# Where the repeated reciprocals of small-head attention are transposed, and in which order the first attention takes its query tiles

## The reference

```
q, k, v = projections of x          # layers 0 and 1: with rotary embedding
scores  = q @ k.T * scale           # layer 1: plus a bias by head and distance
scores  = where(causal, scores, -inf)
out     = softmax(scores) @ v       # per head
x       = layernorm(x + out @ Wo)
```

## Time and profile before

| | us |
|---|---|
| median of 3 runs | 2816.76 |
| the profiled execution's own time | 2823.93 |
| its span, first to last instruction | 2822.2 |
| loop of the first attention (layer 0) | about 30 to 545 |
| loop of the second (layer 1) | about 745 to 1034 |
| loop of the third (layer 2) | about 1262 to 1571 |

### The profile page before, as it was taken

One profiled execution on the slowest core, in us unless ns is written; L12 is line 12 of the kernel. 1 busy time (PEld: TensorE's weight loads), 2 busy tenths in 40 slices (PEclk: granted clock), 3 DMA queues, 4 the chain that ended last, 5 costly groups with the idle time before them and its releaser, 6 DMA issues. The chain is left out here.

```text
span 2822.2 us, 72090 instructions
## 1 busy us (share of the span) xinstructions
PE 2353.0 (83%) x21404; PEld 1825.2 (65%) x21404; DVE 1897.4 (67%) x8141; ACT 1390.2 (49%) x3317; POOL 1385.6 (49%) x1580
## 2 busy tenths in 40 slices
PE   6888888778689980869999799958987999999986
PEld 5666666545366660857777577747775777777755
DVE  4666666656488872657888589955555777767746
ACT  2333333322366650646666456634554666666624
POOL 4666666400366644547778265623332554554501
PEclk9999999989799995989999899989998999999978
DMA  2000000033100011220000100000000000000001
GB/s 73 2 1 0 0 0 0 20 86 79 53 2 0 0 38 42 65 82 2 0 0 0 39 2 1 0 1 2 0 0 23 2 1 0 0 0 0 0 1 31
DMA packets 38281, 45.51 MB, mean 16 GB/s; under 512 B 6160, under 2 KB 28777, under 8 KB 37804
## 3 DMA queue, kind: packets, MB, share of 16 engines
q1 hardware_dynamic: 35820, 38.89, 4.9%
q0 software_dynamic: 2304, 4.79, 0.5%
HBM read 36.62 MB, written 9.74 MB: 16 GB/s over the span
## 5 line engine op out<-in xcount | busy, mean ns | idle before, releaser
L1102 POOL TENSOR_TENSOR a_sm<-a_sm,a_top 128x512 f32<-128x512 f32 x512 | 524.2, 1041 | 279.9 <-DVE a_top L900 278.0
L1025 ACT ACTIVATE a_pr<-a_sm 128x512 f32<-128x512 f32 x512 | 315.2, 626 | 239.8 <-POOL a_sm L1102 151.6
L900 DVE CUSTOM_DVE_ANT_0 a_sm<-bank,cst 128x256 f32<-128x256 f32 (+1 forms) x1024 | 301.0, 353 | 106.3 <-PE bank L762 104.2
L776 PE MATMUL bank<-cst,a_pr 128*128 128x128 f32 x2304 | 309.5, 276 | 1.3 <-ACT a_pt L1035 0.9
L2907 POOL TENSOR_TENSOR a_pr<-a_sm,a_rden 128x512 f32<-128x512 f32 x192 | 197.4, 1049 | 228.1 <-DVE a_rden L2693 227.7
L776 PEld LDWEIGHTS bank<-cst,a_pr 128*128 128x128 f32 x2304 | 257.0, 141 | 33.5 <-issue 23.6
L908 DVE COPY a_pt<-bank 128x512 f32<-128x512 f32 x272 | 186.7, 686 | 132.5 <-PE bank L776 132.4
L1035 ACT ACTIVATE a_pt<-bank 128x512 f32<-128x512 f32 x304 | 177.3, 589 | 87.9 <-PE bank L776 83.9
L2667 DVE CUSTOM_DVE_ANT_0 a_sm<-bank,cst 128x256 f32<-128x256 f32 (+1 forms) x512 | 149.9, 354 | 52.4 <-PE bank L2554 45.1
L796 PEld LDWEIGHTS bank<-a_pt,a_v 128*32 128x32 f32 x4608 | 119.6, 110 | 99.9 <-issue 89.1
L796 PE MATMUL bank<-a_pt,a_v 128*32 128x128 f32 x4608 | 156.5, 276 | 17.8 <-issue 6.9
(11 more groups left out here) (493 smaller groups left out, 5982.8 us busy)
## 6 DMA issues: line engine op xcount, KB each, us to landing
f_spread<-gate_rows SPq DMA_DIRECT2D x16, 512.0 KB, 7.0
W<-in_l_w SPq DMA_DIRECT2D x2, 2048.0 KB, 9.9
x_sorted<-in_l_blank SPq DMA_DIRECT2D x4, 660.0 KB, 7.4
f_xin<-x_sorted SPq DMA_DIRECT2D x10, 264.0 KB, 2.8
X<-in_x SPq DMA_DIRECT2D x4, 512.0 KB, 7.7
a_bias<-bias_rows SPq DMA_DIRECT2D x1, 2048.0 KB, 7.5
X<-y_rows SPq DMA_DIRECT2D x8, 256.0 KB, 5.3
out_x<-X SPq DMA_DIRECT2D x8, 256.0 KB, 2.3
```

The lines of the kernel that those rows point to most:

```text
L776: mm = pe.transpose(tbank[j % 2][:, c * P:(c + 1) * P], pr[j][:, c * P:(c + 1) * P], ident)
L900: ins = dve.tensor_tensor_reduce(sm[j][:, m * kw:(m + 1) * kw], sbank[j][:, m * kw:(m + 1) * kw], mk, 1.0, 3.0e38, ALU.add, ALU.min, top[: ...
L1025: act.activation(pr[j][:, :], sm[j][:, :], ACT.Exp, scale=-1.0).then_inc(S["probs"], 1)
L1102: pool.tensor_tensor(whole, whole, top[:, qt, a:a + m].unsqueeze(2).to_broadcast([P, m, kw]), ALU.subtract).then_inc(S["shifted"], 1)
```

## The change

Three edits. (1) With one lane (layers 1 and 2) the repeated reciprocals are transposed into `PRE` instead of score bank 1 or 0. The scores there no longer wait for `normed`; the step does, whose matmuls write `PRE`. (2) Layer 0 takes the two late quads of a sequence first and the early one last; `second` is the quad at which its second tile begins, and `tile_of` gives which rows of X a finished tile belongs to. (3) The rotary steps of layer 0 come in the order q q k k q q k k, and its first quad waits for only four additions of its sequence, the second quad for all eight.

```diff
@@ class Narrow
+        early, late = [(0, heads, P) for heads in early], [(1, heads, SEQ) for heads in late]
+        self.units = late + early if late_first else early + late
+        self.late_first = late_first
-        self.first_late = len(early) // 4
+        self.second = len(late if late_first else early) // 4
@@ L0_HEADS
+    late_first=True)
@@ narrow_stage
         def end_of(e):
-            return (e // 2) * NQ + (hd.first_late - 1, NQ - 1)[e % 2]
+            return (e // 2) * NQ + (hd.second - 1, NQ - 1)[e % 2]
-        def r_bank(e):
-            if lanes == 2:
-                return 2
-            slot_of = lambda k, lag: end_of(k) + lag
-            here = end_of(e % 2) + LRT
-            return d_bank if not any(slot_of(k, LD) == here for k in range(-4, 8)) else y_bank
+        RB = sbank[2] if lanes == 2 else PRE
+        assert lanes == 2 or NS == NQ
+        def tile_of(e):
+            return e ^ 1 if hd.late_first else e
@@ scores
-                if q == 0:
-                    steps.wait_q_and_k(pe, S, 2 * i + b)
+                steps.wait_q_and_k(pe, S, 2 * i + b, q)
...
-                pe.wait_ge(S["normed"], total(i, 4, begun(s, LRT)) + CREDIT)
+                if lanes == 2:
+                    pe.wait_ge(S["normed"], total(i, 4, begun(s, LRT)) + CREDIT)
@@ values
-                if q in (0, hd.first_late):
-                    pe.wait_ge(S["gathered"], total(i, 4, s // NQ * 2 + qt) + CREDIT)
+                if q in (0, hd.second):
+                    pe.wait_ge(S["gathered"], total(i, 4, s // NQ * 2 + (q > 0)) + CREDIT)
@@ repeat_turn
-                masks_done(i, s, r_bank(e))
+                if lanes == 2:
+                    masks_done(i, s, 2)
+                else:
+                    pe.wait_ge(S["step_out0"], total(i, 2 * NS, NS + (s if in_loop(i) else 0)) + CREDIT)
...
-                    mm = pe.transpose(sbank[r_bank(e)][:, k * P:(k + 1) * P], rx[:, k * P:(k + 1) * P], ident)
+                    mm = pe.transpose(RB[:, k * P:(k + 1) * P], rx[:, k * P:(k + 1) * P], ident)
@@ step (PE)
+                    slot_here = b * NQ - NQ + j * NQ // NS
                     if j % lanes:
-                        masks_done(i, b * NQ - NQ + j * NQ // NS, 0)
+                        masks_done(i, slot_here, 0)
+                    if lanes == 1:
+                        pe.wait_ge(S["normed"], total(i, 4, begun(slot_here + 1, LRT)) + CREDIT)
@@ norm (DVE): reads RB;  residual, tile_stats, tile_aggregate (DVE): index e -> tile_of(e)
@@ class LatentNarrow
-        self.kinds = ["rms", "cq", "ck"] + ["q"] * 4 + ["k"] * 4 + ["v"]
+        self.kinds = ["rms", "cq", "ck"] + ["q", "q", "k", "k"] * 2 + ["v"]
-    def wait_q_and_k(self, pe, S, seq):
-        pe.wait_ge(S["k_ready"], seq + 1 + CREDIT)
-        pe.wait_ge(S["rope_added"], 8 * (seq + 1) + CREDIT)
-        pe.wait_ge(S[self.out_of(1)], self.nth_out(seq, 1) + CREDIT)
+    def wait_q_and_k(self, pe, S, seq, q):
+        if q == 0:
+            pe.wait_ge(S["k_ready"], seq + 1 + CREDIT)
+            pe.wait_ge(S["rope_added"], 8 * seq + 4 + CREDIT)
+            pe.wait_ge(S[self.out_of(1)], self.nth_out(seq, 1) + CREDIT)
+        if q == 1:
+            pe.wait_ge(S["rope_added"], 8 * seq + 8 + CREDIT)
```

More of the change, by code:

```diff
@@ L523, with __init__ @@
     H = 16
-    def __init__(self, dv, per, early, late, place, column):
+    def __init__(self, dv, per, early, late, place, column, late_first=False):
         self.dv, self.per, self.place, self.column = dv, per, place, column
@@ L528, in __init__ @@
         self.cols = self.blocks * P
-        self.units = [(0, heads, P) for heads in early] + [(1, heads, SEQ) for heads in late]
+        early, late = [(0, heads, P) for heads in early], [(1, heads, SEQ) for heads in late]
+        self.units = late + early if late_first else early + late
+        self.late_first = late_first
         self.quads = len(self.units) // 4
-        self.first_late = len(early) // 4
+        self.second = len(late if late_first else early) // 4
         self.at = {}
@@ L573 @@
     place=lambda h: (h % 4 * 32, 32, h // 4, h // 4),
-    column=lambda h: (h // 8, h % 4, h // 4 % 2))
+    column=lambda h: (h // 8, h % 4, h // 4 % 2),
+    late_first=True)
 L1_HEADS = Narrow(
@@ L917, in norm @@
                 dve.wait_ge(S["projected"], 4 * i + e + CREDIT)
-                dve.tensor_tensor(on[:, :], osb[e % 2][:, :], sbank[r_bank(e)][:, 0:cols], ALU.mult).then_inc(S["normed"], 1)
+                dve.tensor_tensor(on[:, :], osb[e % 2][:, :], RB[:, 0:cols], ALU.mult).then_inc(S["normed"], 1)
             def residual(i, e):
                 dve.wait_ge(S["projected"], 4 * i + e + 1 + CREDIT)
-                epilogue.dve(dve, core, B, S, i, e, x_tile(4 * i + e), YB[:, 0:DM])
+                epilogue.dve(dve, core, B, S, i, e, x_tile(4 * i + tile_of(e)), YB[:, 0:DM])
             def tile_stats(i, e):
@@ L928, in tile_stats @@
                 carry_waits(core, dve)
-                dve.bn_stats(B["stat"][:, :], x_tile(t)).then_inc(S["stats"], 1)
+                dve.bn_stats(B["stat"][:, :], x_tile(4 * i + tile_of(e))).then_inc(S["stats"], 1)
             def tile_aggregate(i, e):
@@ L935, in tile_aggregate @@
                 carry_waits(core, dve)
-                dve.bn_aggr(B["mv"][:, e % 4, :], B["stat"][:, :]).then_inc(S["aggregated"], 1)
+                dve.bn_aggr(B["mv"][:, tile_of(e) % 4, :], B["stat"][:, :]).then_inc(S["aggregated"], 1)
             def keep_moments(i, e):
@@ L1202, in alloc @@
         B["tt"] = [sb(f"tt{i}", [P, 2, SEQ]) for i in range(2)]
-    def wait_q_and_k(self, pe, S, seq):
+    def wait_q_and_k(self, pe, S, seq, q):
+        if q:
+            return
         pe.wait_ge(S["k_ready"], seq + 1 + CREDIT)
@@ L1313, in alloc, with chunk @@
         S["diagonal"] = sem("diagonal")
+    def chunk(self, j):
+        return self.kinds[:j].count(self.kinds[j])
     def copy_x(self, pool, core, B, S, b, seq):
@@ L1337, in pe @@
             return mm
-        c = self.rank(j) % 4 * P
+        c = self.chunk(j) * P
         w = F["q"][:, P + c:P + c + P] if kind == "q" else weight(core, 0, "l0_wkrope")[:, c:c + P]
@@ L1370, in pool @@
             pool.wait_ge(S[self.out_of(j)], self.nth_out(seq, j) + CREDIT)
-            r = self.rank(j)
-            tt = B["tt"][r % 2]
+            tt = B["tt"][self.rank(j) % 2]
             dst = B["q"][b] if kind == "q" else B["kx"][b]
-            pool.tensor_tensor(dst[:, r % 4, :], tt[:, 0, :], tt[:, 1, :], ALU.add).then_inc(S["rope_added"], 1)
+            pool.tensor_tensor(dst[:, self.chunk(j), :], tt[:, 0, :], tt[:, 1, :], ALU.add).then_inc(S["rope_added"], 1)
 def l1_attention(core, ctx, next_weights=()):
```

## The result

The changed kernel takes 2866.64 us (median of 4 runs, 2865.94 to 2869.91) against 2817.95 us before: **48.7 us slower**, ratio 1.0177 with a 95% interval of 1.0164 to 1.0189. The forecast was 2853 us, +36.6, with a range of 2836 to 2866. The direction was right, and so was the main mechanism; the price was 12 us too low, and the time lies 0.6 us outside the range.

What follows compares the result with a forecast made beforehand. Prediction: slot lengths set by PE and DVE handing each other score banks, with PE waiting for the norm or POOL. Layers 1 and 2 +51.6 and layer 0 -15 gave +36.6 on 2816.8, so 2853 us; range 2836 to 2866.

Steps and rivals of the forecast that it cites:

- the main mechanism: Layers 1 and 2: PE runs its list in order, so scores queue behind a step that now waits for the norm; +51.6 us.
- The wait moved to the step: Layers 1 and 2, slots with a norm: scores start after the norm and also after the step, formerly run during PE's wait.
- layer 2's price: Layer 2, steps q and v behind the norm: 0.95 us each, 1.90 us a sequence, times 15 = 28.5 us.
- The size in layer 1: Layer 1, steps q and v behind the norm: 0.96 + 0.58 = 1.54 us a sequence, times 15 = 23.1 us.
- no cover: Layer 1: DVE was free when the scores came, so it hides at most a few hundredths of a microsecond; taken as none.
- the sum: Whole kernel: -15 us for layer 0 and +51.6 us for layers 1 and 2 give +36.6 us.
- What would come earlier is nothing: Layers 1 and 2: PE's queue blocks earlier scores, and `repeat_turn` freed from masks still waits for the norm; no gain.
- Layer 0: Late quads first and new rotary order: -0.65, -0.32 and 0 us in three slots, -1.0 us a sequence, -15 us in all.
- The slot of the early tile: Layer 0, last slot in the new order: POOL wait goes, DVE's masks and residual set the end; scores 0.65 us earlier.
- The clock: Rival: layers 1 and 2 grow more idle and part runs at 1.2 GHz; perhaps +15 us, 2868 us; chance 4%.
- The upper end: Whole kernel: 2866 us, the top of the range, from part bounds +57.6 (layers 1 and 2) and -6 (layer 0).
- part 1's upper bound of 57.6: Layers 1 and 2, reciprocals' bank: +57.6 us if a step's first matmul after a stall costs 0.1 us more.

## Why the prediction was right and where it was wrong

**The wait moved to the step: right.** The step's last place in PE's list puts the scores behind it. The run with the wait alone shows it without anything else changed, and gives layer 2's price to within 0.05 us. The Trainium skill's rule that matmuls stay in program order (TensorE: Matmul & The Clock Gate, Step-by-step: what each phase is for; the section that the prediction names has the weight loads that are pulled forward) holds in every row above: no scores start before the step in front of them.

**The size in layer 1 is in part luck.** +1.60 us a sequence against 1.54 is a mean of +1.43 and +1.76. The steps hold the scores for 1.68 us (1.06 and 0.62), 0.14 more than was taken. The sequences of the short kind still grew by 1.43 only, so about 0.25 us was covered, where the prediction took no cover. And every second sequence pays 0.3 us for the loop's turn, which was not in the sum.

**"What would come earlier is nothing": off by little at most.** Edit 1 as a whole has sequences 0.15 us shorter in layer 2 than the wait alone.

**Layer 0: right in each slot, within 0.3 us.** The slot of the early tile came out 0.28 us longer than worked out in one sequence and 0.10 in the next. Of 24.7 us of POOL wait, dropping the wait for the last four additions gave 0.70 us a sequence: DVE's norm and residual stand right behind it (0.20 and 0.30 us of idle time for them in the rows above). The tile order brought the remaining 0.19; that this is the masks' new place is not shown apart.

**The step that failed is "The clock", and with it the first turns, which the sum left out (next paragraph).** I named the clock as a rival with 4% and put it at nothing in the sum, by a share of busy time: "Layer 0 has 86% at a clock of 1.00, so I see no reason for a fall". A share of busy time doesn't say how the idle time is cut. Layer 1's wait of 1.68 us, which the sum itself gave (0.72 + 0.96), brought the clock to 1.2 GHz in four steady sequences (6.4 us) and in the one with the first turn (about 1.3 us, 23.19 against 21.84 to 21.91 without a fall); behind the 3.38 us of idle time in layer 0 a sixth fall cost about 1.6. That is about 9.3 of the 12.1 us that were missing. With the idle time ahead of step q filled, the four were gone. Layer 0's waits of 1.5 to 1.7 us in steady state kept the clock at 1.00, so the length of a wait alone doesn't decide either; what does stays open.

**The first turn of each loop was not in the sum at all.** Steady state was multiplied by 15. The sequence with the first turn exceeds a steady one by 4.9 us in layer 0 (0.1 before), 3.5 in layer 1 (1.7) and 2.0 in layer 2 (1.1), together +7.4 us. 2.9 of them are the two falls of the clock just counted, 4.5 are new. The sum against the forecast is then 9.3 for the clock, 4.5 for the first turns, 0.8 for a steady sequence of layer 0 that gained 0.89 instead of 1.0 us, -0.2 in the rest of layer 1 and -2.3 in the rest of layer 2 (1.75 instead of 1.90 us a sequence): 12.1.

What sets the delays of the first turn is open. PE's rows say "issue"; DMA queues of kind instruction moved 6 packets between 96 and 104 us, but 5 in the kernel before too; a shift of the code by 32 instructions did nothing; and one kernel had the delay in one execution and not in the other. That it is the fetch of instructions is only argued.

**The ends of the range.** The upper end doesn't follow from its own terms: 2816.8 + 57.6 - 6 is 2868, not 2866, and 2866.64 lies inside that. That would have been luck: layers 1 and 2 lost 58.2 us, and part 1's upper bound of 57.6 was meant for dearer steps, which were not what was missing. The +15 us for the clock had no working behind it.

## What to carry to other kernels

Before a wait is moved from one instruction to another on the same engine, read what stands between them in that engine's list: an instruction that filled the idle time of a wait becomes its tail when it has to wait itself. Look at the length of a longer wait as well as at the engine's share of busy time: here the clock of TensorE fell, in some sequences, behind one idle stretch of 1.7 us in a stage in which PE was busy 85%. Price the first turn of a loop apart from the steady ones. And where two engines hand banks to each other in a fixed order, look for the first idle time in a slot, not the longest: one exchange in PE's list gave four times what the whole change of order had given.

## What the runs showed of the hardware

- TensorE's granted clock fell to 1.2 GHz for about 3.4 us behind an idle time of 1.68 us, not each time: in 4, 2, 2, 5 and 1 of 13 steady sequences in five profiles with the same idle time, and in none in the one where eight transposes cut it to 0.36 us. Each of these falls cost 1.6 us. Idle times of 1.5 to 1.7 us in the steady state of another stage, busy 86 to 88%, brought none.
- Behind an idle time of 3.1 to 3.5 us at a loop's first turn the clock fell in five profiles of six.
- Four matmuls of 256 columns hold the next group 0.1 us longer when they start behind a wait: 1.05 to 1.06 us against 0.95 to 0.96.
- The turn of a loop of two sequences costs about 0.3 us where PE has no wait there, and nothing where it waits for the norm anyway (19.57 and 19.90 us in turn, against 18.14 and 18.14).
- The first turn of a loop of this size costs 0.1 to 5 us more than the others. In layer 0 3.1 to 3.5 us of "issue" came with the new order each time, where the kernel before had a wait of 1.7 us for POOL; with the old order 2.75 us came in one profile of six.
